# The key mask of three attention layers: added by TensorE in PSUM before, by VectorE in its maximum after

## The reference

```python
# layers 0 and 3 ("latent"): 16 heads of 32; keys are 128 context tokens and the 128 queries' own tokens
attn = einsum('bkhd,bnhd->bhkn', q, kmat) / DH
full_mask = concatenate([attention_mask.astype(bool), ones((b, k_len), bool)], axis=-1)
attn = softmax(where(full_mask[:, None, None, :], attn, -inf))
out = rmsnorm(attn_out @ out_w + out_b + residual);  MLP 512 -> 2048 -> 512 with gelu, plus residual
# layer 1 ("gqa"): 32 query heads of 16 over 8 key heads, 128 keys, a mask for each query and key
attn = softmax(einsum('bkgld,bksd->bkgls', q, k) * scale + encoder_attention_mask);  out proj, layer norm
# layer 2 ("cross"): 16 heads of 32, 128 context keys, a mask for each key
attn = softmax(where(mask[:, None, None, :], scores, finfo.min));  out proj, layer norm, MLP
```

## Time and profile before

| | us |
|---|---|
| runs, three | 2555.38, 2555.6, 2562.81 |
| median | 2555.6 |
| profiled execution, its own time | 2562.53 |
| its span, first to last instruction | 2560.7 |
| TensorE busy | 2452.8 (96%) |
| VectorE busy | 1231.4 (48%) |
| ScalarE busy | 1085.6 (42%) |
| GpSimd busy | 1120.2 (44%) |
| mask matmuls, 320 | 277 ns the shortest |

### The profile page before, as it was taken

One profiled execution on the slowest core, in us unless ns is written; L12 is line 12 of the kernel. 1 busy time (PEld: TensorE's weight loads), 2 busy tenths in 40 slices (PEclk: granted clock), 3 DMA queues, 4 the chain that ended last, 5 costly groups with the idle time before them and its releaser, 6 DMA issues.

```text
span 2560.7 us, 48767 instructions
## 1 busy us (share of the span) xinstructions
PE 2452.8 (96%) x18464; PEld 2053.4 (80%) x18464; DVE 1231.4 (48%) x3296; ACT 1085.6 (42%) x3712; POOL 1120.2 (44%) x1972
## 2 busy tenths in 40 slices
PE   7999998999999999998888999999999999899999
PEld 6888886888888878886777788888888888788887
DVE  4555655332224667766666332243455556432332
ACT  4555554111114787777767111111455555311111
POOL 2453545600053787778876630033344443730000
PEclk9999999999999999998988999999999999999999
DMA  4111312211033233223443320122021111320100
GB/s 162 59 59 59 104 55 79 83 50 50 1 109 126 74 106 121 96 97 125 150 161 121 115 91 1 50 87 74 26 88 63 51 43 61 114 87 1 50 33 17
DMA packets 106774, 198.07 MB, mean 77 GB/s; under 512 B 8304, under 2 KB 35632, under 8 KB 103600
## 3 DMA queue, kind: packets, MB, share of 16 engines
q1 hardware_dynamic: 106544, 194.97, 23.1%
HBM read 136.22 MB, written 58.72 MB: 76 GB/s over the span
## 4 chain that ended last, share of the span: by engine, by line
PE 79%; ACT 11%; DVE 5%; POOL 3%; issue 1%; DMA 1%; SPq 0%; DVEq 0%; POOLq 0%
PE banks L326 70%; ACT plain_high L731 5%; PE banks L467 5%; PE banks L497 3%; ACT plain_low L731 2%; POOL plain_high L1342 2%; ACT plain_work L796 1%; DVE stats L1134 1%; PE banks L521 1%; ACT plain_work L715 1%; DVE plain_work L1149 0%; DMA plain_high<-attention_w 0%; DVE plain_high L1004 0%; ACT plain_low L715 0%; DVE rounded_low L1053 0%
## 5 line engine op out<-in xcount | busy, mean ns | idle before, releaser
L326 PE MATMUL banks<-rounded_work,rounded_low 128*128 128x512 f32 (+1 forms) x2688 | 534.3, 355 | 11.5 <-DVE rounded_low L1166 9.5
L326 PEld LDWEIGHTS banks<-rounded_work,rounded_low 128*128 128x128 f32 x2688 | 445.3, 198 | 76.8 <-issue 15.9
L982 ACT ACTIVATE plain_work<-banks,columns 128x512 f32<-128x512 f32 x192 | 132.4, 690 | 870.8 <-PE banks L326 870.8
L326 PE MATMUL banks<-rounded_work,rounded_high 128*128 128x512 f32 (+1 forms) x2400 | 483.4, 355 | 2.1 <-DMA rounded_work<-ctx_split 1.7
L326 PEld LDWEIGHTS banks<-rounded_work,rounded_high 128*128 128x128 f32 x2400 | 396.6, 191 | 68.2 <-issue 6.2
L1342 POOL TENSOR_SCALAR plain_high<-plain_high,inv_sum 128x128 f32<-128x128 f32 (+1 forms) x768 | 296.6, 409 | 317.5 <-DVE inv_sum L1026 317.2
L1318 DVE CAST rounded_work<-plain_work 128x512 fp32r<-128x512 f32 x192 | 105.3, 549 | 685.7 <-ACT plain_work L982 674.9
L326 PE MATMUL banks<-rounded_low,rounded_work 128*128 128x512 f32 x1728 | 414.9, 391 | 0.0
L326 PE MATMUL banks<-rounded_high,rounded_work 128*128 128x512 f32 (+1 forms) x1728 | 390.2, 377 | 0.0
L326 PEld LDWEIGHTS banks<-rounded_low,rounded_work 128*128 128x128 f32 x1728 | 321.6, 188 | 68.6 <-issue 2.8
L326 PEld LDWEIGHTS banks<-rounded_high,rounded_work 128*128 128x128 f32 x1728 | 309.1, 188 | 60.5 <-issue 1.4
(11 more groups left out here) (106 smaller groups left out, 3120.9 us busy)
## 6 DMA issues: line engine op xcount, KB each, us to landing
plain_work<-x SPq DMA_DIRECT2D x96, 256.0 KB, 3.2
plain_work<-mlp_w SPq DMA_DIRECT2D x96, 256.0 KB, 2.7
rounded_work<-ctx_split SPq DMA_DIRECT2D x16, 1024.0 KB, 6.0
u<-plain_work SPq DMA_DIRECT2D x48, 256.0 KB, 2.8
plain_work<-u SPq DMA_DIRECT2D x12, 1024.0 KB, 7.2
x<-plain_work SPq DMA_DIRECT2D x48, 256.0 KB, 2.3
plain_work<-attention_w SPq DMA_DIRECT2D x44, 256.0 KB, 2.6
ctx_split<-rounded_work SPq DMA_DIRECT2D x8, 1024.0 KB, 5.6
```

The costliest lines, as they stand in the source:

```text
L326: mm = pe.matmul(dst, lhs(i), rhs(j), start=first and n == 0, stop=last and n == 2, skip_group_check=True)
L982: act.activation(gelu[:, j % 2, :], bank(key), ACT.Gelu_apprx_tanh, bias=col(y, 28 + j)).then_inc(evac_of(key), 1)
```

## The change

In layers 0, 2 and 3 the mask is added as in layer 1: VectorE adds it per segment in the operation that takes the maximum and writes the negated masked scores to SBUF, frees the bank, and the exponential reads SBUF. TensorE's mask matmuls go, and its wait for the mask; VectorE waits for it at the first bank of a pair. The mask is loaded onto all 128 partitions; its bf16 tile has a second half of zeros, so that a latent segment of 256 keys (128 masked, 128 not) takes one operation. The constants change, and the work area grows by 1 KB a partition.

```diff
@@ pe_scores
-                    mm = three_passes(pe, dst, lambda h: QT[part, h, c, b * P:(b + 1) * P], key_t, i == 0, y.kind == GQA and i == n_blk - 1)
-                    if y.kind == GQA and i == n_blk - 1:
+                    mm = three_passes(pe, dst, lambda h: QT[part, h, c, b * P:(b + 1) * P], key_t, i == 0, i == n_blk - 1)
+                    if i == n_blk - 1:
                         mm.then_inc(s_filled[r], 1)
-            if y.kind != GQA:
-                pe.wait_ge(mask_ready, mask_index(y, p) + 1)
-                for r in range(4):
-                    part = slice(32 * r, 32 * r + 32)
-                    dst = PS[:, r, :].rearrange("p (i n) -> p i n", i=n_blk)[:, :, 0:P]
-                    pe.matmul(dst, ones_row[part, :], mask_row[part, p % 2, b, :].unsqueeze(1).broadcast_to([32, n_blk, P]),
-                              start=False, stop=True, skip_group_check=True).then_inc(s_filled[r], 1)
@@ act_exp
-            if y.kind == GQA:
-                act.wait_ge(s_free[r], y.use(p, k) + 1)
-            else:
-                act.wait_ge(maxed, 4 * (R if y.n == 0 else R - L[1].rounds) + r + 1)
+            act.wait_ge(s_free[r], y.use(p, k) + 1)
...
-                last = act.activation(pr[:, r, part], pr[:, r, part] if gqa else PS[:, r, part], ACT.Exp, scale=-1.0 if gqa else 1.0,
-                                      bias=neg_max[:, R % 2, r, g:g + 1],
+                last = act.activation(pr[:, r, part], pr[:, r, part], ACT.Exp, scale=-1.0, bias=neg_max[:, R % 2, r, g:g + 1],
                                       accum_out=row_sum[:, R % 2, r, g:g + 1])
-            last.then_inc(exped if y.kind == GQA else s_free[r], 1)
+            last.then_inc(exped, 1)
@@ dve_max
+            if k == 0 and r == 0 and y.kind == GQA:
+                dve.wait_ge(qk_loaded[p % 2], 16 * (p // 2 + 1))
+            elif k == 0 and r == 0:
+                dve.wait_ge(mask_ready, mask_index(y, p) + 1)
             dve.wait_ge(s_filled[r], u + 1)
...
-            dve.tensor_reduce(neg_max[:, R % 2, r, 0:y.segs], src.rearrange("p (g n) -> p g n", g=y.segs), AX.X, ALU.max,
-                              negate=True).then_inc(maxed, 1)
+            pr = prob(y)[R % 2]
+            for g in range(y.segs):
+                part = slice(g * y.seg, (g + 1) * y.seg)
+                mask = qk_mask[:, p % 2, b, :] if y.kind == GQA else mask_row[:, p % 2, b, 0:y.seg // P, :].rearrange("p x n -> p (x n)")
+                last = dve.tensor_tensor_reduce(pr[:, r, part], PS[:, r, part], mask, -1.0, 3.0e38, ALU.add, ALU.min, accum_out=neg_max[:, R % 2, r, g:g + 1])
+            last.then_inc(s_free[r], 1)
@@ dve_mask, sp_mask
-            dve.tensor_scalar(mask_row[:, p % 2].rearrange("p b n -> p (b n)"), src, 0.0, MASKED, ALU.is_equal, ALU.mult).then_inc(mask_ready, 1)
+            dve.tensor_scalar(mask_row[:, p % 2, :, 0, :], src.rearrange("p (b n) -> p b n", b=2), 0.0, MASKED,
+                              ALU.is_equal, ALU.mult).then_inc(mask_ready, 1)
-            sp.dma_start(dst[0:P:32, :], src[2 * p:2 * p + 2].rearrange("b n -> (b n)").unsqueeze(0).broadcast_to([4, 2 * P])).then_inc(mask_loaded, 16)
+            sp.dma_start(dst, src[2 * p:2 * p + 2].rearrange("b n -> (b n)").unsqueeze(0).broadcast_to([P, 2 * P])).then_inc(mask_loaded, 16)
```

More of the change, by code:

```diff
@@ L78, in sem @@
             return ctx.enter_context(nc.semaphore(name))
-        C_KB = 76
+        C_KB = 77
         with nc.sbuf_tensor("plain_low", [P, 8 * 2048], F32) as plain_low, \
@@ L118, in build @@
         wide_bias = work(plain, 68, D)
-        mask_row = plain[2][:, 70 * KB:71 * KB].bitcast(BF16).rearrange("p (h b n) -> p h b n", h=2, b=2)
-        mask_i32 = plain[2][:, 71 * KB:72 * KB].bitcast(I32)
-        mask_u8 = plain[2][:, 71 * KB:71 * KB + 64].bitcast(U8)
+        mask_row = plain[2][:, 70 * KB:72 * KB].bitcast(BF16).rearrange("p (h b x n) -> p h b x n", h=2, b=2, x=2)
+        mask_i32 = plain[2][:, 76 * KB:77 * KB].bitcast(I32)
+        mask_u8 = plain[2][:, 76 * KB:76 * KB + 64].bitcast(U8)
         raw = work(plain, 72, 2, D)
@@ L146, in build @@
         cols = sb("columns", [P, 4, 44], F32)
-        ones_row = sb("ones_row", [P, P], BF16)
         neg_max = sb("neg_max", [P, 2, 4, 4], F32)
@@ L181, in build @@
         hi_done = sem("hi_done")
-        ident_zero, ones_zero, ident_done, consts, cols_loaded = sem("ident_zero"), sem("ones_zero"), sem("ident_done"), sem("consts"), sem("cols_loaded")
-        maxed, exped, inverted, normed = sem("maxed"), sem("exped"), sem("inverted"), sem("normed")
+        ident_zero, ident_done, consts, cols_loaded = sem("ident_zero"), sem("ident_done"), sem("consts"), sem("cols_loaded")
+        exped, inverted, normed = sem("exped"), sem("inverted"), sem("normed")
         mask_loaded, mask_ready = sem("mask_loaded"), sem("mask_ready")
@@ L723, in act_exp @@
             pr = prob(y)[R % 2]
-            if y.kind == GQA:
-                act.wait_ge(s_free[r], y.use(p, k) + 1)
-            else:
-                act.wait_ge(maxed, 4 * (R if y.n == 0 else R - L[1].rounds) + r + 1)
+            act.wait_ge(s_free[r], y.use(p, k) + 1)
             for g in range(y.segs):
                 part = slice(g * y.seg, (g + 1) * y.seg)
-                gqa = y.kind == GQA
-                last = act.activation(pr[:, r, part], pr[:, r, part] if gqa else PS[:, r, part], ACT.Exp, scale=-1.0 if gqa else 1.0,
-                                      bias=neg_max[:, R % 2, r, g:g + 1],
+                last = act.activation(pr[:, r, part], pr[:, r, part], ACT.Exp, scale=-1.0, bias=neg_max[:, R % 2, r, g:g + 1],
                                       accum_out=row_sum[:, R % 2, r, g:g + 1])
-            last.then_inc(exped if y.kind == GQA else s_free[r], 1)
+            last.then_inc(exped, 1)
         def act_heads(act, y, p, k):
@@ L994, in dve_max @@
             R, u = y.round(p, k), y.use(p, k)
-            dve.wait_ge(s_filled[r], u + 1)
[L996 to L1007, removed]
-            dve.tensor_reduce(neg_max[:, R % 2, r, 0:y.segs], src.rearrange("p (g n) -> p g n", g=y.segs), AX.X, ALU.max,
-                              negate=True).then_inc(maxed, 1)
+            b = of_round(y, k)[0]
+            if k == 0 and r == 0 and y.kind == GQA:
+                dve.wait_ge(qk_loaded[p % 2], 16 * (p // 2 + 1))
+            elif k == 0 and r == 0:
+                dve.wait_ge(mask_ready, mask_index(y, p) + 1)
+            dve.wait_ge(s_filled[r], u + 1)
+            pr = prob(y)[R % 2]
[4 more added lines that the diff above has]
+            last.then_inc(s_free[r], 1)
         def dve_copy(dve, key, dst):
@@ L1018, in dve_invert @@
         def dve_invert(dve, y, p, k):
-            R, u = y.round(p, k), y.use(p, k)
+            R = y.round(p, k)
             for half in range(2):
[L1021 to L1025, removed]
+                dve.wait_ge(exped, 4 * R + 2 * half + 2)
                 dve.reciprocal(inv_sum[:, R % 2, 2 * half:2 * half + 2, 0:y.segs],
@@ L1800, in sp_mlp @@
             store(GROUPS - 1)
-        N_CONSTS = 4 + 2 + 2 + 1
+        N_CONSTS = 4 + 2 + 1 + 1
         block = ctx.enter_context(nc.Block())
@@ L1827, in _ @@
         def _(dve):
[L1828 to L1833, removed]
+            dve.memset(mask_row[:, :, :, 1, :].rearrange("p h b n -> p (h b) n"), 0.0).then_inc(consts, 1)
             dve.wait_ge(cols_loaded, 16)
```

## The result

| us | before | changed kernel |
|---|---|---|
| median of 6 runs | 2555.49 | 2567.95 |
| lowest to highest | 2554.51 to 2562.81 | 2566.31 to 2570.07 |
| profiled execution, its own time | 2562.53 | 2566.31 |
| its span | 2560.7 | 2564.2 |

The account below looks back on a forecast made before the run. TensorE was busy 2452.8 of 2560.7 us, with some layer 2 rounds bound by ScalarE. Latent layers -4.8, layer 2 +6.7 and clock +1.5 gave +3.4 us: 2559.0 from the median 2555.6, range 2547 to 2568.

Parts of the forecast that it names:

- The forecast's own spread: Whole kernel: 2552 to 2566 us, from the bounds of the 256-column costs and of the clock.
- rival (c): Layer 2's query matmuls: longer TensorE waits keep the clock low, +8.6 us, 2566 in all; chance 0.24.
- a gain of 4.8: Layers 0 and 3: removed mask matmuls outweigh dearer exponentials, -4.7 us, and -0.1 for the first round's masks.
- VectorE has 20 idle us in a latent pair: VectorE's dearer maxima, 0.36 us a latent round, hide in idle time except where the first maximum is on the chain.
- The 0.36 us: Latent rounds: VectorE's maxima grow by 0.09 us a bank, 0.36 a round, bounded by -0.7 and +1.0.
- VectorE's work holds up a latent round: Layers 0 and 3: an observation named as showing the forecast wrong; no size given.
- rival (d): Layer 2: VectorE becomes late, its 1.0 us a round against 10 us idle; no separate chance given.
- the mask is worth 0.11 us a latent round: TensorE, layers 0 and 3: scores to transposes shrink from 1.05 to 0.94 us, judged by layer 1's maskless scores.
- the 0.24 us step in the timeline: TensorE, latent round: time from masks to transposes, taken as the upper end of what a mask is worth.
- the split of the next inputs swallows the gain of one round in four: Layer 0: TensorE waits for VectorE's split in the fourth round, which gains nothing and pays 0.05 us.
- layer 2, +6.7: Layer 2: ten rounds of longer exponentials +6.5 us, first maxima +0.75, earlier transposes -0.5.
- +1.5 of the clock: Layer 2's query matmuls: longer waits lower TensorE's granted clock, 0.25 us a pair, bounded by -5 and +9.

Follow-up runs that it names:

- the early copy: Changed kernel with VectorE's copy of the fourth transposed bank moved ahead of its fourth maximum in layers 0 and 3; 2559.56 us, ratio 1.0010.
- the rounds without any mask: Kernel before with the key mask left out in layers 0, 2 and 3, maxima and exponentials unchanged; 2548.33 us, ratio 0.9966.
- the best of both: Layers 0 and 3 as changed, with VectorE's fourth copy ahead of its fourth maximum; layer 2 as in the kernel before; 2553.33 us, ratio 0.9983.
- the latent half: The change in layers 0 and 3 alone, layer 2 as in the kernel before; 2559.44 us, ratio 1.0008.
- layer 2 alone: The change in layer 2 only, layers 0 and 3 as in the kernel before; 2566.01 us, ratio 1.0034.

## Why the prediction was right in one half and wrong in the other

The time fell inside the range by luck. The forecast's own spread ended at 2566; the rest of the upper range fits rival (c), a clock that makes it 2566, and that did not come. What filled most of the 9 us above the forecast was a loss of 3.7 us in the latent layers, which the forecast had as a gain of 4.8.

*Wrong: "VectorE has 20 idle us in a latent pair ... so this hides but where the first maximum is itself on the chain".* This is the step that failed. It set an average idle time against the cost and asked only for the maxima's own readers. Behind the fourth maximum on the same queue stands a copy, and TensorE's value products wait for it. Its slack before was 0.24 and 0.11 us in two rounds of a pair. The 0.36 us (sized right: steps of 0.345 us, at 161.56 and 161.90 for one) plus TensorE's own gain of 0.12 used it up. In two rounds of four in each latent pair the value products came 0.25 and 0.38 us later; less the mask's gain, the rounds went from 12.53 to 12.63 and from 15.23 to 15.50 us, the third went from 9.65 to 9.53, and the pair of layer 0 went from 50.06 to 50.33, that of layer 3 from 50.86 to 51.13. The gain was turned into a new wait, and the early copy alone brought it back. The prediction named this observation as one that would refute it ("VectorE's work holds up a latent round"), but gave it no price: rival (d) looked at layer 2 only. Forecast -4.8 for the latent layers, -1.7 and -3.1 of it in the stretches of the table; measured +1.9 and +1.8 us there.

*Right: the mask is worth 0.11 us a latent round.* It is 0.13 us in a round of the kernels with VectorE's mask and the early copy, 12.53 to 12.40, and 0.09 to 0.15 in the rounds without any mask. The comparison with layer 1's maskless scores found it; the 0.24 us step in the timeline was the trap.

*Right: the split of the next inputs swallows the gain of one round in four.* That round of layer 0 stays at 12.65 to 12.67 us.

*Right in mechanism, a little large: layer 2, +6.7 and +1.5 of the clock, 8.2 in all.* In the stretch of the table, which leaves out 0.65 of it, the mean of four profiles is 210.7 against 204.9 of five with TensorE's mask, +5.9 us (+6.6 between the two kernels' own profiles). Exponentials are 0.384 us apart, as forecast from layer 1. In a middle pair the first round (8.96 us before) and the second up to the query matmuls (7.80) take 16.76 us together before and 9.05 + 8.29 = 17.34 now: +0.58, for a forecast of 0.65 - 0.08. Writing to PSUM in place of SBUF gives 0.04 us an exponential back, takes 0.04 a segment on VectorE, and returns 3.9 of the 5.9 us. The SBUF source is the larger part of the loss in layer 2, and ScalarE its bound, as read from the chain. The masks gave back 0.06 us a pair, as forecast: the 0.23 that their absence alone is worth is used up by VectorE's dearer first maximum, which the chain now goes through.

*The clock.* The granted clock in layer 2, windows with columns as in the earlier trace rows, is 0.92 in the kernel before:

```profile
1180.00:1392.00 212.00, 184.79 (x2139) 158.42 (x2139) 136.28 (x339) 150.80 (x675) 166.09 (x338) 0.92 0.41 140
```

0.89 in the changed kernel:

```profile
1180.00:1392.00 212.00, 179.57 (x2028) 153.40 (x2020) 149.19 (x740) 152.50 (x641) 158.94 (x329) 0.89 0.42 141
```

Of TensorE's two levels, 1.2 and 2.4 GHz, it has the lower one for longer, and it waits for longer. The 48 query matmuls of the last six pairs take 7.61 and 7.69 us on average in the changed kernel's two profiles, 7.43 and 7.46 in those of before: 0.2 us a pair, 1.2 in all. The first pair varies by itself: 6.00 and 6.94 us before, 7.49 and 6.92 in the changed kernel. Over all profiles the seven sets add up to 52.9 us with VectorE's mask to SBUF and to 51.6 with TensorE's, +1.3, but the best of both, with TensorE's mask there, has 53.1. So the +1.5 is borne out on average and not clear of the spread from profile to profile; rival (c)'s +8.6 did not come.

*Not forecast:* layer 1 is 0.9 us shorter.

*What stays open.* Stretches of the table add up to +1.9 + 1.8 + 5.9 - 0.9 = 8.7 us, the medians say 12.5. For the latent half they agree (2.8 and 2.5). For layer 2 alone they don't: +5.0 in the stretches, +9.0 in the median (interval 5.6 to 12.0), and the kernel with the early copy has 0.1 and 2.6 (0.3 to 4.9). For the whole change the 8.7 us lie within the interval of the medians, 7.7 to 14.3. No profile shows where more could lie: what a span holds outside the four stretches is 1409 to 1413 us in the four profiles with VectorE's mask to SBUF in layer 2, and 1407 to 1417 in the other nine. Whether executions that were not profiled lose some 3 us more there stays open.

## What to carry to other kernels

Before idle time is set against added work, list what stands behind that work on the same engine's queue, and the slack of each of its readers: a quarter of a microsecond or so, 28 times, turned a gain into a loss here, beside 20 idle us in each pair. When an operation is taken off the bounding engine, that engine also arrives earlier at what follows, so subtract the gain from the slacks too. The step that the mask matmuls own in the timeline, 0.24 us, was worth 0.13 when they went; the same sequence without them elsewhere in the program had given 0.11.

## What the runs showed of the hardware that was not expected

From the end of VectorE's copy to the start of the dependent matmuls there were 0.42 us (162.93 to 163.35), and the profile books the 0.20 us for which TensorE was idle as issue, not as a wait for VectorE. A reader who looks for "<-DVE" rows alone misses it.

The masked maximum costs 0.21 us for 128 columns with an SBUF target, 0.25 with PSUM, and 0.345 for 256 columns. The exponential of 256 columns from SBUF is 0.49 us after the last (147.34 - 146.84 = 0.50 and 151.68 - 151.19 = 0.49), 0.45 from PSUM before: 0.04 us more, as at 128 columns. The Trainium skill (VectorE: DVE Perf Modes, section on the TRN2 errata) has it as fixed cycles per instruction, and both widths agree with that now.

Two executions of one kernel with clock means of 0.982 and 0.985 differed by 8 us, nearly all of it in three short stretches. A profile is one draw: compare it stage by stage.
